# Causal mask written by ScalarE, a longer lag and new places, in a fused attention and expert kernel

## What is computed

```
g = -softplus(x @ Wg.T + bg);  lam = softplus(x @ Wdl.T + Lparam);  G = cumsum(g, axis=1)
scores = einsum('bthd,bshd->bhts', q, k) * scale
decay  = exp(where(t >= s, G[t] - G[s], -inf))
lamw   = lam at level(t - s)
y      = einsum('bhts,bshd->bthd', scores * decay * lamw, v)
out    = layernorm(y @ Wo.T + x) * ln_g + ln_b ;  x = x + out
gate   = softmax(layernorm(x) @ fWg + fbg), top 2, normalised
x      = x + sum over experts of gate * (layernorm(x) @ We.T + be)
```

## Time and profile before

| | us |
|---|---|
| median of 3 runs | 1553.94 (1553.23 to 1556.63) |
| the profiled execution | 1553.5 |
| its span | 1551.7 |
| TensorE / ScalarE / VectorE / GpSimd busy | 1442.8 / 1165.8 / 1026.5 / 883.1 |

### The profile page before, as it was taken

How to read it: one execution, slowest core, us unless ns; L and a number is a source line. 1 busy time by engine, 2 the same in 40 slices (tenths; PEclk the granted TensorE clock), 3 DMA queues, 4 the chain that set the end, 5 groups by cost and what they waited for, 6 DMA issues and landing times.

```text
span 1551.7 us, 30846 instructions
## 1 busy us (share of the span) xinstructions
PE 1442.8 (93%) x10614; PEld 1213.8 (78%) x10678; DVE 1026.5 (66%) x2483; ACT 1165.8 (75%) x3351; POOL 883.1 (57%) x879
## 2 busy tenths in 40 slices
PE   5699999999999999999999999998999999999976
PEld 4488887878878788788878788787887878888863
DVE  5355656686656767577665866668665676656677
ACT  2589887887788777787778877788778877777740
POOL 1064557745585456944578455864458545695561
PEclk8699999999999999999999999999999999999996
DMA  5311111111110111101111011111111011111100
GB/s 182 62 11 16 40 17 31 14 25 37 21 24 16 28 32 37 17 7 39 24 34 16 17 30 23 37 15 24 38 20 24 16 23 24 37 17 17 22 8 14
DMA packets 256486, 44.12 MB, mean 28 GB/s; under 512 B 197976, under 2 KB 254666, under 8 KB 256202
## 3 DMA queue, kind: packets, MB, share of 16 engines
q1 hardware_dynamic: 255484, 41.90, 14.3%
q10 hardware_dynamic: 846, 0.25, 0.1%
HBM read 32.38 MB, written 9.18 MB: 27 GB/s over the span
## 4 chain that ended last, share of the span: by engine, by line
PE 65%; ACT 12%; POOL 10%; DVE 7%; issue 2%; SPq 2%; DMA 1%; ACTq 0%; POOLq 0%; DVEq 0%
PE o_ps L1330 17%; PE l_ps L1261 9%; PE s_ps L1245 7%; PE s_ps L1247 7%; PE s_ps L1246 7%; ACT w_all L707 6%; PE aux L1245 5%; POOL a_lo L586 5%; PE aux L1246 5%; PE aux L1247 5%; ACT a_hi L729 2%; DVE a_all L903 2%; POOL yn L611 2%; PE o_ps L1325 1%; DVE z L979 1%
## 5 line engine op out<-in xcount | busy, mean ns | idle before, releaser
L586 POOL TENSOR_TENSOR a_lo<-a_all,a_hi 128x512 fp32r<-128x512 f32 (+2 forms) x640 | 710.7, 1126 | 569.1 <-ACT a_hi L729 566.5
L707 ACT ACTIVATE w_all<-l_ps,bias 128x128 f32<-128x128 f32 x2304 | 631.2, 389 | 50.4 <-PE l_ps L1261 49.3
L903 DVE TENSOR_TENSOR a_all<-s_ps,w_all 128x512 f32<-128x512 f32 (+3 forms) x768 | 424.0, 554 | 364.5 <-PE s_ps L1247 348.1
L729 ACT ACTIVATE a_hi<-a_all 128x512 fp32r<-128x512 f32 (+2 forms) x640 | 363.9, 590 | 200.7 <-DVE a_all L903 198.5
L1330 PE MATMUL o_ps<-a_hi,v_all 128*128 128x512 f32 (+2 forms) x1280 | 467.1, 369 | 17.0 <-POOL a_lo L586 16.5
L1245 PE MATMUL s_ps<-q_hi,xt_hi 128*128 128x512 f32 (+3 forms) x768 | 289.0, 376 | 4.2 <-DVE a_all L903 4.1
L1330 PEld LDWEIGHTS o_ps<-a_hi,v_all 128*128 128x128 f32 x1280 | 242.9, 190 | 63.0 <-POOL a_lo L586 31.2
L1247 PE MATMUL s_ps<-q_hi,xt_lo 128*128 128x512 f32 (+3 forms) x768 | 268.3, 349 | 0.0
L1246 PE MATMUL s_ps<-q_lo,xt_hi 128*128 128x512 f32 (+3 forms) x768 | 268.2, 349 | 0.0
L1330 PE MATMUL o_ps<-a_lo,v_all 128*128 128x512 f32 (+2 forms) x640 | 230.9, 361 | 0.0
L1261 PE MATMUL l_ps<-rb,mask 96*128 96x112 f16 (+4 forms) x1792 | 146.4, 222 | 23.7 <-ACT w_all L707 23.7
(11 more groups left out here) (179 smaller groups left out, 2015.2 us busy)
## 6 DMA issues: line engine op xcount, KB each, us to landing
rb<-eb_scratch SPq DMA_DIRECT2D x1016, 0.8 KB
ra<-ea_scratch SPq DMA_DIRECT2D x512, 4.0 KB, 2.0
mt<-m_scratch SPq DMA_DIRECT2D x62, 128.0 KB, 2.1
nt<-n_scratch SPq DMA_DIRECT2D x62, 128.0 KB, 2.6
tx<-in_L_attn_x SPq DMA_DIRECT2D x9, 512.0 KB, 4.3
...
```

What stands on the lines that cost most here:

```text
L586: pool.tensor_tensor(a_lo[r][:, 0:t1 - t0], a[r][:, 0:t1 - t0], a_hi[r][:, 0:t1 - t0].bitcast(F32), ALU.subtract).then_inc(a_lo_done, 1)
L707: last = act.activation(w[k][:, W_AT[j] + dd, :].rearrange("p (f c) -> p f c", f=2), l_tiles[:, :, :, i - i0], ACT.Exp, bias=bias[b % 2][: ...
L729: act.activation(a_hi[r][:, 0:t1 - t0], a[r][:, 0:t1 - t0], ACT.Copy).then_inc(a_hi_done, 1)
L903: dve.tensor_tensor(a[(n * NG + g) % NA][:, 0:t1 - t0], s_ps[:, g % 2, 0:t1 - t0], w[n % 2][:, at:at + (t1 - t0) // P, :].rearrange("p i n ...
```

## The change

The two mask products go. Instead ScalarE copies `negm` (now float32, keys by queries, each value eight times) over both l_ps banks after the last exps of a head (`preset_mask`), and the level products of unit 0 accumulate onto it; TensorE's unit 0 waits for the new semaphore `masked`. For that the banks must have been written by TensorE on all columns before, which two products at the start see to (`open_banks`) and, for later heads, the order of the units: the one that fills all of l_ps is last now. Lag 5 and six buffers of a, a_hi, a_lo in place of 4 and five. Mean and variance within the loop move from VectorE to GpSimd, in seven operations. All places are new. After the loop, products whose result nobody reads stand behind four of the last pieces. The DMA scratch of the program is set to 8192.

```
-UNITS = [[(0, 0, 8)], [(1, 1, 7)], [(2, 2, 6)], [(3, 3, 5), (5, 5, 3)], [(4, 4, 4)]]
+UNITS = [[(0, 0, 8)], [(1, 1, 7)], [(2, 2, 6)], [(4, 4, 4)], [(3, 3, 5), (5, 5, 3)]]
-LAG = 4
+LAG = 5
-U_AT = {0: 0, 3: 1, 5: 2, 7: 3, 10: 4}
-Q_AT = {5: 0, 20: 1}
-V_AT = {11: 0, 27: 1, 40: 2, 46: 3}
+U_AT = {0: 0, 2: 1, 4: 2, 6: 3, 7: 4}
+Q_AT = {5: 0, 16: 1}
+V_AT = {8: 0, 27: 1, 39: 2, 44: 3}
+PE_MORE = {17: [('Y', 0)], 28: [('Y', 1)], 82: [('T', 0)], 98: [('T', 1)], 106: [('Z', 0)], 130: [('Z', 1)],
+           134: [('X', 0)], 136: [('X', 1)], 144: [('L', 0)], 162: [('H', 0)], 192: [('G', 0)], 198: [('H', 1)],
+           221: [('EL', 0)], 230: [('H', 2)], 233: [('H', 3)], 236: [('EL', 1)], 241: [('H', 4)], 269: [('H', 5)],
...
+DVE_MORE = {17: [('t_stat', 1)], 20: [('t_stat', 2)], 21: [('o', 1), ('t_stat', 0)], 24: [('t_stat', 3)],
+            29: [('stat1', 1)], 44: [('stat1', 0)], 48: [('stat1', 3)], 56: [('stat1', 2)], 85: [('t_low', 0)],
...
+            168: [('gate', 2)], 173: [('gate', 3), ('up', 0)], 189: [('softplus', 0), ('softplus', 1)],
+            192: [('guard', 0)], 193: [('sums', 0)], 200: [('log', 0)], 209: [('log', 1)], 220: [('decay', 0)],
...
+ACT_MORE = {17: [('y', 0)], 26: [('y', 1)], 44: [('t_apply', 2)], 62: [('t_apply', 3)], 77: [('t_high', 0)],
+            98: [('t_high', 1)], 108: [('apply2', 0)], 129: [('x_high', 0)], 136: [('x_high', 1)], 144: [('num', 0)],
+            148: [('abs', 0)], 166: [('exp', 0)], 177: [('ln', 0)], 189: [('lnl', 0)], 220: [('l_high', 0)],
+            238: [('l_high', 1)]}
+POOL_MORE = {24: [('t_dev', 0)], 29: [('t_apply', 1)], 32: [('xb', 0)], 44: [('dev1', 0)],
+             48: [('apply1', 0), ('apply1', 1), ('t_apply', 0)], 56: [('apply1', 3)],
+             64: [('apply1', 2), ('scale', 0), ('scale', 1)], 72: [('add', 0)], 76: [('xb', 1)], 84: [('add', 1)],
+             89: [('dev2', 0)], 93: [('apply2', 3)], 101: [('apply2', 1)], 124: [('apply2', 2)], 296: [('total', 0)],
+             380: [('total', 1)]}
...
+        def pool_mean_var(pool, b, stats, mv, ve, s_st, s_mv, s_ve):
+
+            base = b * MEAN_VAR
+            pool.wait_ge(s_st, NC * (b + 1))
+            pool.tensor_tensor(mv[:, 1, :], stats[:, :, 1], stats[:, :, 4], ALU.add).then_inc(s_mv, 1)
+            pool.tensor_tensor(mv[:, 3, :], stats[:, :, 2], stats[:, :, 5], ALU.add).then_inc(s_mv, 1)
+            pool.wait_ge(s_mv, base + 2)
+            pool.tensor_scalar(mv[:, 0, :], mv[:, 1, :], -0.5, None, ALU.mult).then_inc(s_mv, 1)
+            pool.tensor_scalar(mv[:, 5, :], mv[:, 3, :], 1.0 / D, EPS, ALU.mult, ALU.add).then_inc(s_mv, 1)
+            pool.wait_ge(s_mv, base + 4)
+            pool.tensor_tensor(mv[:, 2, :], stats[:, :, 1], mv[:, 0, :], ALU.add).then_inc(s_mv, 1)
+            pool.wait_ge(s_mv, base + 5)
+            pool.tensor_tensor(mv[:, 4, :], mv[:, 2, :], mv[:, 2, :], ALU.mult).then_inc(s_mv, 1)
+            pool.wait_ge(s_mv, base + MEAN_VAR)
+            pool.tensor_tensor(ve[:, :], mv[:, 4, :], mv[:, 5, :], ALU.add).then_inc(s_ve, 2)
...
+                def preset_mask(n):
+
+                    act.wait_ge(*((w_done, NU * n) if n else (l_open, 1)))
+                    if n == 0:
+                        act.wait_ge(s_consts, 2)
+                    act.activation(l_ps[:, :, :].rearrange("p f (c i) -> p f c i", i=NC),
+                                   negm[:, :].rearrange("p (f c) -> p f c", f=2)[:, :, :, None].broadcast_to([P, 2, HF, NC]),
+                                   ACT.Copy).then_inc(masked, 1)
...
                         if place % 4 == 2 and g in U_AT and n + 1 < NH:
                             exps(n + 1, U_AT[g])
+                            if U_AT[g] == NU - 1 and n + 2 < NH:
+                                preset_mask(n + 2)
...
-                    if n or u:
+                    if u == 0:
+                        pe.wait_ge(masked, n + 1)
+                    else:
                         pe.wait_ge(w_done, n * NU + u)
-                    started = [False, False]
+                    started = [u == 0, u == 0]
...
-                        if d == 0:
-                            for f in range(2):
-                                last = mm(f, l_bank[f], negm[:, :],
-                                          identb[:, f * HF:(f + 1) * HF, :])
...
+                def open_banks():
+
+                    for f in range(2):
+                        last = pe.matmul(l_ps[:, f, :], c("ident"), c("ident")[:, None, :].broadcast_to([P, 4, P]), start=True, stop=True,
+                                         skip_group_check=True)
+                    last.then_inc(l_open, 1)
...
+                pe.wait_ge(a_done, NH * NG)
+                idle = {("Y", 1): 30, ("X", 0): 8, ("X", 1): 5, ("H", 1): 12}
                 for kind, n, i in LAST_PIECES[1:]:
                     piece(kind, n, i)
+                    for _ in range(idle.get((kind, i), 0)):
+                        pe.matmul(s_ps[:, 1, :], mask[:, 0:P], mask[:, 0:4 * P], start=True, stop=True,
+                                  skip_group_check=True)
```

More of the change, by code:

```diff
@@ L104, in constants @@
     put("m10", np.broadcast_to(l_b[:, 0] == 10, (KB, P)))
-    put("neg", row[None, :] > row[:, None])
     put("ident", row[None, :] == row[:, None])
@@ L143, in program @@
         main_stage(nc, x, Wq, Wk, Wv, Wg, bg, Wdl, Lparam, Wo, ln_g, ln_b, fWg, fbg, fWe, fbe, masks, table, out,
-                   m_dram, n_dram, ea_dram, eb_dram, cst, mask, m, c, negm, identb, identr, rows,
+                   m_dram, n_dram, ea_dram, eb_dram, cst, mask, m, c, negm, identr, rows,
                    wet_hi, wet_lo, fwg2, wcat_hi, wcat_lo)
 MEAN_VAR = 6
-LAG = 4
+LAG = 5
 NA = LAG + 1
@@ L311, in main_stage @@
         wot = a_all[:, 0:WD]
-        ones, neg, minus = (first_use(at, P) for at in (4 * WD, 4 * WD + P, 3 * WD))
+        ones, minus = (first_use(at, P) for at in (4 * WD, 3 * WD))
         wcr_t, fwg = first_use(4 * WD + 2 * P, NLOG), first_use(4 * WD + 2 * P + NLOG, E)
@@ L337, in main_stage @@
         ra_in, rb_in, m_in = ([sem(f"{n}{k}") for k in range(2)] for n in ("ra_in", "rb_in", "m_in"))
-        l_mm, w_done, zeroed = sem("l_mm"), sem("w_done"), sem("zeroed")
+        l_mm, w_done, masked, zeroed = (sem(n) for n in ("l_mm", "w_done", "masked", "zeroed"))
+        l_open = sem("l_open")
         s_mm, a_done, a_hi_done, a_lo_done = sem("s_mm"), sem("a_done"), sem("a_hi_done"), sem("a_lo_done")
@@ L828, in _ @@
                 token_ln(0)
+                preset_mask(0)
                 act.wait_ge(s_wot, 1)
@@ L1106, in more @@
                             token_statistics(b + 1, 2 * i)
-                        if kind == "t_mean" and b + 1 < B:
-                            token_mean(b + 1)
                         if kind == "t_low" and b + 1 < B:
```

54 lines of the change are left out of this document (20 added, 34 removed), and 16 rows, old and new, of tables (DVE_MORE, PE_MORE, POOL_MORE).

## The result

The changed kernel takes 1543.45 us (median of 4, 1541.97 to 1544.45), the kernel before 1553.94: a ratio of 0.9931, interval 0.9916 to 0.9946. It is faster by 10.5 us, not by 38, and lies 2.5 us above the forecast range.

The account below looks back on a forecast made before the run. TensorE's own work was taken to bound some 94% of a batch. Gains of 28.4 (masks), 5 (full batches), 2 (last batch), 1.25 and 1.5 (tail) made 38 us, giving 1516 us, range 1499 to 1541.

Parts of the forecast that it names:

- Heads 3 and 4: Heads 3 and 4 of a full batch: losses beside the masks fall to 3.9 us from 5.9.
- the wait before the decay sums: Head 3, place 192: the decay sums' inputs are ready 2.6 us after TensorE gets there.
- the slow clock behind that wait: Heads 3 and 4: after a wait over 2 us, perhaps the slow clock again, 1.4 us.
- The mask products: TensorE, each head: dropping two identity products saves 0.45 us in 63 heads of the loop, 28.4 us.
- The copy: ScalarE, once per head: a 128x1024 mask copy takes 1.02 us, hidden and counted at nothing.
- The slack near 1.2: Even head: the mask copy ends at 17.5 us, TensorE starts unit 0 at 18.7; slack 1.2 us.
- The lag: Values five groups behind, with an extra buffer: worth nothing itself, hides the copy, about 0.6 us a head without it.
- Statistics on GpSimd: Heads 0 to 2 of a full batch: with three chains of 2.1 us on GpSimd, TensorE loses 6.5 us, against 5.3.
- the largest lateness: Heads 0 to 2: TensorE loses the largest lateness of GpSimd's a_lo, 59.2 us for 52.7, so 6.5 us.
- GpSimd clogs: Rival: mean-and-variance chains past 2.1 us lose time one to one; at 5 us a chain, 1568 us; chance 0.05.
- The last batch: Last batch: no token pieces on GpSimd, 5.8 us less pile-up, taken as 2 us gained.
- Batch 0 and the tail: Batch 0: no gain beside the masks. After the loop: 1.25 us from moving total(1), 1.5 from filler matmuls.

Follow-up runs that it names:

- mask_pe: The changed kernel with the two mask products of each head back on TensorE and no mask copy on ScalarE; 1556.73 us.
- stats_dve: The changed kernel with means and variances back on VectorE, each right behind the last statistics it needs; 1523.01 us.
- mask_pe_stats: The changed kernel with the mask products back on TensorE, no mask copy, and means and variances back on VectorE; 1545.62 us.

## Why the prediction was wrong

In the profiled executions the kernel gained 9 us where the sum had 38. Of the 29 missing, 6 are batch 0, 12 the six full batches, 9 the last batch and 2 the tail.

- **Heads 3 and 4 (3.9 for 5.9).** The step that cost most in the full batches: 2.0 us a batch were to be gained beside the masks, and on average nothing was (49.2 us for 50.1, of which the masks are 0.86). The parts came as I said: seven table loads went, and the wait before the decay sums was 2.3 us in a full batch (2.6 forecast). TensorE's idle time in the two heads fell from 4.1 to 3.2 (batch 4). But I took the slow clock behind that wait at half its price (0.7 of 1.4), and it came at 1.5 in four batches, at twice that in one and not at all in one. The 0.9 of shorter idle time did not come out as length: 0.3 went to more time at half clock (3.4 us a batch for 2.8), and where the rest went no run shows. Of the wait itself I had half: VectorE frees the bank of a v piece 0.1 us before the sums' inputs are ready. Filling the stall is worth 4.7 us.
- **The mask products (28.4).** The 0.45 us was right at full clock (0.42). "63 heads" failed in heads 1 and 2, where GpSimd sets the pace: they give nothing back, so a full batch gains 2.4 us at full clock instead of 3.6. It did not fail in heads 3 and 4: their pauses keep their length, and the products spared between them count. With the statistics off GpSimd, all eight heads give it and the mask is worth 22.6 us. Heads 5 to 7 fell by 0.3 each against the kernel before and by 0.4 against mask_pe, as the new places made them 0.1 longer.
- **The copy.** Right: 1.028 us for 1.02, one wait of 2.9 us for it in all. The slack near 1.2 is there in heads 6 and 7 only. I laid out a single head without pieces and took it for all; a second copy costs up to 1.0 us in the others.
- **The lag.** I called it worth nothing itself and 38 us by hiding the copy; without it the kernel takes 56 more. How much of that is GpSimd's pile-up rather than the copy stays open.
- **Statistics on GpSimd (6.5 for 5.3).** For heads 0 to 2 of the full batches the sum came out (66.1 us for 66.6), but by luck: two errors cancelled. Each chain takes about 1.9 us, and the rows of 0.20 to 0.25 were met; yet taking the chains back gives 2.0 us a batch in heads 1 and 2, against 1.2 more for the whole stretch. What made up for it, the lag and the new places, I had at nothing here: in stats_dve these heads are 1.4 us shorter than before, the masks left out. The waits for a_lo were 3.0 us a batch and not 5 to 7, so the largest lateness is not what TensorE waits. By the two runs the move costs 18.7 and 20.4 us. It does so the way the rival "GpSimd clogs" says, but not under its condition, chains over 2.1 us, and not one to one: 3.7 us less work gave 2.0.
- **The last batch (2 us gained beside the masks).** It lost 3.6. Most stands in head 2, which took 23.9 us for 19.3 with the clock at 0.93; with the statistics back on VectorE the batch takes 150.0 for 153.5. That it has no token pieces did not keep GpSimd's pile-up out of it.
- **Batch 0 and the tail.** Batch 0 lost 2.1 us instead of none beside the masks; in head 4 TensorE waits 3.7 us for the decay inputs, and the clock falls behind it. In mask_pe batch 0 takes 162.8 us, in mask_pe_stats 167.0, with head 4 at 21.7 and 24.6: much of this is the clock. Of the tail's 2.75 us only 0.4 came; the idle products ended 4.4 us too early.

Two things cut across these parts. The statistics are in the last batch, in heads 1 and 2 and in the mask term at once, so their 19 to 20 us don't add to the others. And executions of one kernel differ by how often the clock falls: the changed kernel has 38.0 us at half clock in the loop against 21.2 before. Why it falls in one batch and not in the next, with the same pause ahead of it, stays open. Open, too, is what bounds heads 3 and 4 when the decay sums no longer do; four rearrangements made them longer or left them.
